# Turning and splitting the feed-forward's first block inside the attention's last block, in a Mamba-2 and ternary feed-forward layer on one core

## The reference

```python
x = L0_attn_u
x = _layernorm(x + _L0_attn_ref(x, ...), axis=-1)
x = _layernorm(x + _L0_ffn_ref(x, ...), axis=-1)

# attention (state space): z, x, B, C, dt from one projection; 8 heads of 128
xBC = silu(conv4(xBC));  dt = softplus(dt + bias)
y = ssd(x, dt, A, B, C, D)              # decays, states carried along the sequence
yg = y * silu(z)
yn = yg * rsqrt(mean(yg * yg) + eps) * norm_w
out = yn @ W_out.T

# feed-forward: weights are made ternary (-1, 0, 1 times the mean magnitude)
up, gate = x @ wu.T, x @ wg.T           # 512 -> 2048
out = (silu(up) * gate) @ wd.T          # 2048 -> 512
```

## Time and profile before

| | us |
|---|---|
| median of 3 runs | 1473.99 (1472.82 to 1474.25) |
| profiled execution, its own time | 1469.2 |
| its span | 1467.5 |
| TensorE busy | 1372.1 |
| VectorE busy | 1147.3 |
| ScalarE busy | 799.3 |
| GpSimd busy | 636.7 |

### The profile page before, as it was taken

One profiled execution on the slowest core, in us unless ns is written; L12 is line 12 of the kernel. 1 busy time (PEld: TensorE's weight loads), 2 busy tenths in 40 slices (PEclk: granted clock), 3 DMA queues, 4 the chain that ended last, 5 costly groups with the idle time before them and its releaser, 6 DMA issues.

```text
span 1467.5 us, 27103 instructions
## 1 busy us (share of the span) xinstructions
PE 1372.1 (94%) x9514; PEld 883.9 (60%) x9514; DVE 1147.3 (78%) x1844; ACT 799.3 (54%) x1592; POOL 636.7 (43%) x628
## 2 busy tenths in 40 slices
PE   6897999999999999999977989999999999999997
PEld 3454555555555656556555667676777767677773
DVE  6886787887778878788656887878797978888884
ACT  5685474773756738567364454454454544454440
POOL 0573354573655737446334333343342433333331
PEclk9899999999999999999987999999999999999999
DMA  7455325363453634425361120110101010110001
GB/s 257 111 191 164 111 77 129 85 162 91 95 148 80 155 88 105 137 73 151 112 217 32 37 96 28 44 37 23 59 29 59 30 45 30 44 44 30 27 27 64
DMA packets 138007, 129.11 MB, mean 88 GB/s; under 512 B 40336, under 2 KB 110352, under 8 KB 136592
## 3 DMA queue, kind: packets, MB, share of 16 engines
q1 hardware_dynamic: 137872, 127.35, 29.6%
HBM read 99.93 MB, written 27.39 MB: 87 GB/s over the span
## 4 chain that ended last, share of the span: by engine, by line
PE 35%; DVE 26%; issue 19%; ACT 11%; POOL 4%; DMA 4%; SPq 1%; DVEq 0%; ACTq 0%; POOLq 0%
PE ring L1008 7%; PE ring L810 5%; PE ring L837 5%; PE p_turn L992 4%; PE p_y L992 3%; DVE acc L1642 3%; PE p_seg L992 3%; PE p_st L992 2%; ACT p_seg L1203 2%; ACT xdt L1194 2%; DVE xdt L1949 2%; PE p_y L881 2%; DVE xdt L1957 2%; PE p_y L889 1%; ACT grow L1356 1%
## 5 line engine op out<-in xcount | busy, mean ns | idle before, releaser
L810 PE MATMUL ring<-u_split,weights 128*128 128x512 f16 x1620 | 376.9, 383 | 0.4 <-DVE x_ch L1647 0.4
L810 PEld LDWEIGHTS ring<-u_split,weights 128*128 128x128 f16 x1620 | 155.5, 99 | 171.4 <-issue 9.4
L1560 POOL TENSOR_TENSOR xdt<-xdt 128x512 f32<-128x512 f32 x64 | 81.4, 1273 | 291.0 <-DVE xdt L1957 291.0
L1642 DVE SCALAR_TENSOR_TENSOR acc<-ring,taps,acc 128x511 f32<-128x511 f32 (+2 forms) x192 | 143.7, 748 | 4.5
L837 PE MATMUL ring<-w_out,raw 128*128 128x512 f16 x672 | 147.1, 379 | 0.0
L1194 ACT ACTIVATE xdt<-p_turn,dts 128x128 f32<-128x128 f32 x256 | 73.0, 376 | 88.6 <-PE p_turn L861 88.6
L1469 POOL TENSOR_TENSOR raw<-yg,raw 128x512 f16<-128x512 f32 x64 | 79.4, 1241 | 87.2 <-ACT raw L1224 86.6
L837 PEld LDWEIGHTS ring<-w_out,raw 128*128 128x128 f16 x672 | 65.8, 99 | 77.7
L1464 POOL TENSOR_TENSOR yg<-y_ch,z_ch 128x512 f32<-128x512 f32 x64 | 82.4, 1288 | 58.6 <-DVE y_ch L1762 58.6
L1356 ACT ACTIVATE grow<-xdt,tanh_scale 128x512 f32<-128x512 f32 x64 | 46.2, 722 | 94.8 <-DVE xdt L1949 94.7
L881 PE MATMUL p_y<-seg,xdt 128*128 128x128 f32 x512 | 72.1, 286 | 18.3 <-DVE seg L1740 18.0
(11 more groups left out here) (383 smaller groups left out, 3435.9 us busy)
## 6 DMA issues: line engine op xcount, KB each, us to landing
cum_rows<-cum_dram SPq DMA_DIRECT2D x64, 256.0 KB, 6.5
quant<-in_w_ffn SPq DMA_DIRECT2D x24, 512.0 KB, 4.6
quant<-in_w_ffn SPq DMA_DIRECT2D x48, 256.0 KB, 4.2
u_raw<-in_u_t SPq DMA_DIRECT2D x8, 1024.0 KB, 13.0
cum_g<-cum_dram SPq DMA_DIRECT2D x64, 128.0 KB, 6.9
rows<-in_u_tok SPq DMA_DIRECT2D x32, 256.0 KB, 4.6
x_dram<-rows SPq DMA_DIRECT2D x32, 256.0 KB, 2.0
tern_ug<-quant SPq DMA_DIRECT2D x32, 256.0 KB, 3.5
```

Of the source, the lines that this page charges most:

```text
L810: mm = pe.matmul(bank_k[:, :], w_in[:, ws, k, col:col + P], us[:, par, k * T:(k + 1) * T], start=(i == 0), stop=(i == 3 * KD - 1))
L1560: pool.tensor_tensor(tile_[:, 1, :, :], tile_[:, 0, :, :], tile_[:, 1, :, :], ALU.mult).then_inc(hid_ok, 1)
L1642: dve.scalar_tensor_tensor(acc[:, buf, k + 1:T], own[:, 0:T - 1 - k], taps[:, h, 2 - k:3 - k], acc[:, buf, k + 1:T], ALU.mult, ALU.add).th ...
```

## The change

**The first block is turned in step 7.** On TensorE the four `turn` of block 0 leave the hand-over. Four `turn_first(k)` do the same transposes, into `p_turn`, one after each `chunk_out` at p = 1 of step 7. ScalarE reads them (`turned_first`) into `x_first`, which is the half of `u_hi` and `u_lo` that step 7 doesn't use.

**It is split in step 7.** The seven `x_high` of block 0 stand at p = 1 (j = 0, 1, 2), p = 2 (3), p = 3 (4 and 5) and in the hand-over (6); the `x_low` and the four `x_sum` on VectorE at p = 2 and p = 3, the last `x_low` in the hand-over. Block 0 has the set of buffers that block 1 had, and the other way round (`XS_AT`).

**The hand-over is filled.** TensorE does `last_chunk(0, 0)` and `last_chunk(1, 0)` there (they need heads 0 to 3 of y alone, and the waits say so), and the seven products of q = 0, before and after `outputs`. For q = 0 of block 0 the chain's bank is `ring[0]`. `ffn_step(-1)` starts with q = 1. ScalarE does all four `gated` before it.

**In step -1** the other half chunks stand in q = 1 to 4 (they stood in q = 1 to 5), block 1 is turned in q = 2 and 3 (was 0 and 1) and split in q = 4 to 7 (was 2 to 6), the sums of squares go to q = 2.

**At the start of the program** VectorE makes `w_lo(4)` after head 3's convolution (was before it), and `cb_tanh` and `cb_silu` of block 1 stand in place 2 of step 0 (were before it). SP issues `load_cum(1, 1, 1)` after the first two `load_abs` of step 1 (was before them).

Tables and the chain's bank:

```diff
-USES_LAST = ["x00", "x01", "x10", "x11", "ssq", "x20", "x21", "x30", "x31"]
+USES_LAST = ["x00", "x01", "x10", "x11", "ssq", "t0", "t1", "t2", "t3", "x20", "x21", "x30", "x31"]
...
+X_AT_FIRST = {4: (0,), 5: (1, 2), 6: (3, 4), 7: (5, 6)}
...
+        def p_chain(n, q):
+            return ring[0] if is_at(n, 0) and q == 0 else (p_st, p_seg)[q % 2]
```

SP, in the attention step:

```diff
                     if p == 0:
-                        load_cum(n, par, 1)
+                        if not is_at(n, 1):
+                            load_cum(n, par, 1)
...
                     if first_row is not None:
                         load_abs(first_row + 2)
                         load_abs(first_row + 3)
+                    if is_at(n, 1) and p == 0:
+                        load_cum(n, par, 1)
```

TensorE, in the attention step:

```diff
                         for c in range(1, C):
+                            if is_at(n, NB - 1):
+                                turn_first(c - 1)
                             chunk_out(n - 1, c)
+                    if p == 1 and is_at(n, NB - 1):
+                        turn_first(C - 1)
```

TensorE, in the hand-over:

```diff
             turn_x(NB, 0, 0)
-            turn(0, 0)
+            last_chunk(0, 0)
             turn_x(NB, 0, 1)
-            turn(0, 1)
+            last_chunk(1, 0)
             states(NB, 0)
-            turn(0, 2)
+            pe.wait_ge(tern_in[0], 16)
+            pe.wait_ge(xlo_ok, 7)
+            product(0, 0, 0, 1, True)
+            pe.wait_ge(s1_ok, 1)
+            product(0, 0, 0, 6, False)
+            pe.wait_ge(turn_free, turn_use(NB, "x01") + 1)
+            product(0, 0, 0, 5, True)
             outputs(NB, 0, 0)
-            turn(0, 3)
+            pe.wait_ge(u2_ok, 1)
+            product(0, 0, 0, 7, False)
+            pe.wait_ge(y_ok, NB * H - 1)
+            product(0, 0, 0, 2, True)
+            pe.wait_ge(y_ok, NB * H)
+            product(0, 0, 0, 4, True)
```

TensorE, in `ffn_step`:

```diff
-                    half = 2 * q - 3 if is_at(t, -1) and 1 <= q < 6 else None
+                    first, second = {1: (None, (0, 1)), 2: (None, (1, 1)), 3: ((2, 0), (2, 1)),
+                                     4: ((3, 0), (3, 1))}.get(q, (None, None)) if is_at(t, -1) else (None, None)
```

ScalarE, in the attention step:

```diff
+                    if is_at(n, NB - 1) and p >= 2:
+                        x_high(0, 0, p + 1)
...
+                    if is_at(n, NB - 1):
+                        for j in ((), (0, 1, 2), (), (5,))[p]:
+                            if j == 0:
+                                for k in range(KD):
+                                    turned_first(k)
+                            x_high(0, 0, j)
```

VectorE, at the start of the program:

```diff
-            w_lo(4)
             conv(0, 0, 3)
...
-            magnitude(1)
             dt_first(1, turn_use(0, "dt"))
+            w_lo(4)
+            magnitude(1)
             w_lo(5)
```

VectorE, in the attention step:

```diff
+                    if is_at(n, NB - 1) and p >= 2:
+                        for j in ((0, 1), (4,))[p - 2]:
+                            x_low(0, 0, j)
+                            x_sum((0, 1, None, None, 3)[j])
...
+                    if is_at(n, NB - 1) and p >= 2:
+                        for j in ((2, 3), (5,))[p - 2]:
+                            x_low(0, 0, j)
+                        if p == 2:
+                            x_sum(2)
```

More of the change, by code:

```diff
@@ L530, in rest, with splits_at, turns_at @@
             return (t, q // 2 - 1) if q else (t - 1, C - 1)
+        def splits_at(t, q):
+            return (X_AT_FIRST if is_at(t, -1) else X_AT).get(q, ()) if has_turn(t) else ()
+        def turns_at(t, q):
+            k = q - 2 if is_at(t, -1) else q
+            return k if has_turn(t) and 0 <= k < 2 else None
         def attention_rest(t, q):
@@ L710, in _ @@
             sp.wait_ge(z_full, NB * H)
+            sp.wait_ge(xlo_ok, 7)
             for q in (4, 5):
@@ L906, in _, with turn_first @@
             pe.wait_ge(made, 4)
+            def turn_first(k):
+                if k == 0:
+                    pe.wait_ge(xin_in, 16)
+                pe.wait_ge(turn_free, turn_use(NB - 1, f"t{k}"))
+                for c in range(C):
+                    mm = pe.transpose(p_turn[:, c * P:(c + 1) * P], u_raw[:, c * D + k * P:c * D + (k + 1) * P], ident[:, :])
+                mm.then_inc(turn_full, 1)
             dt_proj(0, 0, 0)
@@ L1589, in ffn_step @@
             def ffn_step(t, par):
-                for q in range(NQ):
+                for q in range(1 if is_at(t, -1) else 0, NQ):
                     before = pair_at(t, par, q, 1)
@@ L1812, in ffn_scales, with x_low, x_sum @@
                 dve.wait_ge(scale_ok, 2)
+            def x_low(n, par, j):
+                dve.wait_ge(xhi_ok, n * 7 + (j + 1))
+                dve.tensor_tensor(xs_lo[par][j], place(n, SPLIT[j]), xs_hi[par][j], ALU.subtract).then_inc(xlo_ok, 1)
+            def x_sum(k):
+                if k == 0:
+                    dve.wait_ge(turn_free, turn_use(NB - 1, "t3") + 1)
+                else:
+                    dve.wait_ge(xt_ok, k)
+                dve.wait_ge(xlo_ok, (1, 1, 4, 2)[k])
+                a_, b_, c_ = SUMS[k]
+                dve.tensor_tensor(place_first[a_], place_first[b_], place_first[c_], ALU.subtract).then_inc(xt_ok, 1)
             dve.memset(ones, 1.0)
@@ L1877, in step @@
                         within(n, par, p, 0)
+                    if first and p == 2:
+                        cb_silu(1, 1, ring[ring_bank("cb", 0)])
                     if not end:
@@ L1931, in _ @@
             run_steps(dve, step)
-            def x_low(n, par, j):
-                dve.wait_ge(xhi_ok, n * 7 + (j + 1))
-                dve.tensor_tensor(xs_lo[par][j], place[SPLIT[j]], xs_hi[par][j], ALU.subtract).then_inc(xlo_ok, 1)
             def summed(n, q, c, kept, kept_ok, j, op):
@@ L2005, in _ @@
             dve.wait_ge(scales_ok, 3)
-            x_low(0, 0, 0)
-            x_sum(0)
-            x_low(0, 0, 1)
-            x_sum(1)
-            x_low(0, 0, 2)
             skip(NB, 1, 0)
             skip(NB, 1, 1)
-            x_low(0, 0, 3)
-            x_sum(2)
-            x_low(0, 0, 4)
-            x_sum(3)
-            x_low(0, 0, 5)
-            x_low(0, 0, 6)
+            summed(0, 0, "c11", s1, s1_ok, 2, ALU.add)
             def ffn_step(t, par):
                 n, own = t + 1, 1 - par
-                for q in range(NQ):
+                for q in range(1 if is_at(t, -1) else 0, NQ):
                     before, earlier = pair_at(t, par, q, 1), pair_at(t, par, q, 2)
```

226 lines of the change are left out of this document (118 added, 108 removed).

## The result

The changed kernel takes 1460.48 us (median of 4 runs, 1459.47 to 1463.34), the one before 1473.46 (1472.82 to 1474.25): a ratio of 0.9915, 95% interval 0.9898 to 0.9932, so 13.0 us or 0.85% less. The forecast was 1457, 17 us less, with a range of 1448 to 1467.

A forecast was written before the change was run, and what follows sets the result against it. TensorE, busy 94% of the span, was taken as the bound, so gains come only where it idles or runs at the lower clock. 10.8 (after step -1) - 0.8 (clock) + 7.0 (start) = 17 us: 1474 to 1457, range 1448 to 1467.

The forecast's parts named there:

- (a): Step 7: the four turns between the chunks only change place, 4 x 0.44 = 1.8 us.
- (b): Step 7, end of p = 1: `turn_x` waits about 0.9 us for ScalarE's read; 1.2 us more in all, between 0 and 3.
- (c): Step 7, places 2 and 3: VectorE's added instructions delay convolutions; first four 3.7 us, 2.4 us lost at `x_dt`, 1.7 at the mask.
- the mask of place 3: Step 7: TensorE's `within` of the second head has no slack and loses 1.7 us waiting for the mask.
- My 0.8 us for the clock: Step -1: taken off the gain because TensorE would be idle some 6 us in q = 5.
- 14.0: Hand-over: q = 0 done 9.65 us earlier, with two half chunks (5.2) and two turns (0.9) less left to do: 14.0 us won.
- (d): Start: `w_lo(4)` moved from ahead of head 3's convolution, which TensorE's mask wait follows; 2.4 us gained, bounds 0 and 4.
- (e): Start: magnitude piece issued ahead of `load_cum`, so ScalarE's 9.43 us wait shrinks; 4.3 us gained, between 0 and 9.43.
- R1: Half the gain: VectorE slower in step -1 (5.7 us less) or piece no earlier (4.3 less); 1462 or 1467; 27% with R4.
- R2: More: splits find VectorE's gaps, step 7 pays 2 us instead of 5.3, piece lands 7 us earlier; 23 us, 1451; 18%.
- R3: Slower: clock falls to 1.2 GHz through places 2 and 3 of step 7, up to 30 us more; 1487 at worst; 5%.
- R4: Hand-over: `xlo_ok` so late that products stand after `outputs` as before, and `outputs` waits too; 12 us, 1462; 27% with R1.

The follow-up runs named there:

- halves_back: Changed kernel with both half chunks taken out of the hand-over, into q = 1 and q = 2 of step -1: 1463.0 us, ratio 0.9924 to before.
- u_mid: Changed kernel with `load_u(2)` issued behind step 1's two magnitude pieces but ahead of `load_cum(1, 1, 1)`: 1457.9 us, ratio 0.9899 to before.
- after_again: The changed kernel, unaltered, timed once more beside later runs: 1459.1 us, ratio 0.9906 to before.
- feed_only: Changed kernel with the start of the program as it was before: 1465.9 us, ratio 0.9945 to before.
- cum_first: Changed kernel with `load_cum(1, 1, 1)` ahead of the magnitude pieces again: 1461.4 us, ratio 0.9915 to before.
- u_late: Changed kernel with the 1 MB `load_u(2)` issued behind step 1's magnitude pieces and `load_cum`, not ahead of `store_cum`: 1454.4 us, ratio 0.9861 to before.
- thin_last: Changed kernel with block 1's splits and sums in step -1 cut to 2 columns of 512 (block 1's result wrong): 1453.4 us, ratio 0.9861 to before.
- start_only: The kernel before with only the start's part of the change: 1467.8 us, ratio 0.9961 to before.
- combo: Changed kernel with the edits of `u_late` and `splits_behind` together: 1453.2 us, ratio 0.9852 to before.
- thin_step7: Changed kernel with block 0's splits and sums cut to 2 columns of 512 (block 0's result wrong): 1457.0 us, ratio 0.9885 to before.
- splits_behind: Changed kernel with step 7's splits and sums behind the second head's convolution, `x_high(3)` and `x_high(4)` behind its tanh: 1455.6 us, ratio 0.9881 to before.

## Why the prediction was right

On the clock of before (2.06 us added to the rows after), step by step:

| step (us) | predicted | after |
|---|---|---|
| step 7 ends (`turn_x` behind the last z tile) | 758.5 | 758.5 |
| half chunk (0, 0) begins | 761.4 | 761.6 |
| half chunk (1, 0) begins | 766.4 | 766.6 |
| product 1 begins | 772.4 | 772.9 |
| `outputs` ends | 779 | 780.6 |
| q = 0 done | 781.6 | 783.3 |
| product 3 in q = 1 | 784.7 | 786.6 |
| in q = 4 | 818.6 | 820.5 |
| in q = 5, 6, 7 | 829.2, 841.9, 850.9 | 831.7, 843.4, 853.5 |
| first of step 0 | 860.2 | 862.5 |

**Step 7.** The sum of 7 us held (6.7). (a) The turns cost their 1.8. (b) `turn_x` waited 0.78 us for ScalarE's read, not 0.9. (c) At place 2 the four instructions took 4.4 us in place of 3.7:

```profile
731.50 0.68 DVE L1893 TENSOR_TENSOR xs_more<-u_split,xs_more 128x512 f16<-128x512 f32 x1
732.28 1.46 DVE L1903 TENSOR_TENSOR u_split<-u_split 128x512 f32<-128x512 f32 x1
733.66 1.75 DVE L1893 TENSOR_TENSOR xs_more<-u_split,xs_more 128x512 f16<-128x512 f32 x1
735.34 0.68 DVE L1903 TENSOR_TENSOR u_split<-u_split 128x512 f32<-128x512 f32 x1
```

```profile
731.69 1.50 POOL L1546 TENSOR_TENSOR raw<-yg,raw 128x512 f16<-128x512 f32 x1 [0.69 <-ACT raw L1277]
733.15 1.71 POOL L1554 TENSOR_TENSOR sq_sum<-sq_sum,sq 128x512 f32<-128x512 f32 x1
```

The two long ones meet two long ones on GpSimd; VectorE's other two took 0.68. I had said that GpSimd has a gap there, and it hadn't. The Trainium skill (SBUF — State Buffer, section "SBUF: two separate sides") has the two engines lock a shared pair of ports, and these rows agree: GpSimd's instructions grow too, from 1.16 and 1.27 us. `x_dt` was late by 2.71 us (2.4 predicted). The trace after shows no wait for the mask of place 3, to which I gave 1.7 us, and a tile slowed by 1.7 us (4.44 for 2.75) in its place. It would be wrong to read this as a term that wasn't there. `halves_back` has the same tile at full clock and then the wait, 1.21 us, and loses the same 6.7 us in sum, so the mask was the limit as I had said, and the lower clock ran beside it.

**The hand-over.** Every start up to product 1 is within 0.5 us. The starts wait for VectorE: z's gate ends at 764.48 and half chunk (1, 0) begins at 764.53, the last split ends at 770.68 and product 1 begins at 770.83. So the 1.5 us that half chunk (0, 0) took longer cost nothing. What failed is the clock behind product 1, for which I let each instruction take its full-clock time. Two products took 0.8 and 0.45 longer, which nothing hid, and with the 0.5 by which product 1 was late they make the delay of 1.6 to 1.9 us that stands from `outputs` to q = 4. My 0.8 us for the clock were for q = 5. So the gain there was 12.3 us, not 14.0.

`u_mid`, which differs only at the start of the program, shows what the step is worth without it, as its products ran at full clock behind the same wait:

```profile
765.91 1.03 PE L1033 MATMUL ring<-xs_more,weights 128*128 128x256 f16 x8 [2.51 <-DVE b_tok L1892]
...
778.38 1.05 PE L1033 MATMUL p_turn<-c_ch,weights 128*128 128x256 f16 x8 [1.37 <-DVE xdt L2046]
```

From product 1 to product 3 of q = 1 that is 12.5 us. I had 12.3 (772.4 to 784.7), the trace after has 13.7, and `after_again`, `feed_only`, `cum_first`, `u_late` and `thin_last`, with the same order there, have 15.1 to 15.3. The term that I left out is worth 0 to 3 us, from one execution to the next.

**Step -1.** That VectorE sets the pace in q = 4 to 7 is shown by `thin_last`, and it gave back 3.8 us against 3.2. The single terms were less good than the sum: from q = 4's product 3 to step 0's first they were 11.2, 11.8, 10.0 and 9.0 us against 10.6, 12.7, 9.0 and 9.3, and in q = 4 TensorE did not wait for VectorE, where I had said every q.

**Net** 8.5 us in the trace and 8.1 by `feed_only`, against 10.8 - 0.8 = 10.0. Reckoned in the same way, five more traces with this order give 6.6 to 9.8, and the 9.8 is `u_mid`'s.

**The start** gained 5.8 us by `start_only`, predicted 7.0, but by other terms. (d) I took 2.4 us. At 109.03 of before, ahead of the long wait, the lead is 2.2 in the trace after, 3.4 in `start_only`'s and 3.5 in `cum_first`'s, and 1.7 to 4.4, 3.2 on average, in all twelve traces with this start: some 0.8 us more than I took. (e) I took 4.3. The traces give 2.7: TensorE's wait for `x_dt` was 8.9, 9.1 and 9.6 us in the three with `load_cum` first, and 4.6 to 7.8, 6.5 on average, in the eight with the piece first. The timed runs of `cum_first` give 0 to 1.3 and can't decide. The step that failed says that the piece's way "is as long at worst (less was moved ahead of it)". It was longer in seven traces of eight, by 2 us on average; that the `load_cum` issued just ahead of it is the reason is argued, not shown. With 3.2 and 2.7 the sum is 5.9, and 5.8 was measured: a term too small and one too large made my 6.7, and that the sum was near is in part luck. The sign that I named for it, a wait of 5 us or less on ScalarE, came in none of the eight (5.09 to 8.36, 7.65 in the trace after).

**The rivals.** R1 (half) holds in part, as the piece came less early than I took, and the median of 1460.5 lies at the upper end of the forecast's own 1453 to 1461, just below R1's 1462; its other half, 12 us each in q = 6 and 7, didn't come (10.0 and 9.0). R2 didn't come, as step 7 paid 6.7 us. R3 didn't come: the clock in places 2 and 3 fell to 0.95 only, and that cost nothing at the end of step 7. R4 didn't either: `xlo_ok` came 2.51 us late, and `outputs` didn't wait.

## What to carry to other kernels

Filler work on an engine goes behind the instruction that the critical path waits for, not ahead of it: moved behind the convolution (and ScalarE's part behind the tanh), the whole splits cost no more, up to product 1, than splits cut to two columns ahead of it. When work is moved into idle time, a step behind a wait of 2.5 us has two prices, at full and at the lower clock, and belongs in the sum as a range; where another engine's instruction comes later anyway, the slow clock is free. And a load that is late is moved by what stands in the queue ahead of it: look for the large load that delays a small store on which others wait. A stretch that DMAs set is priced from several traces, since one trace here was off by 2 us and more.

## What the runs showed of the hardware

ScalarE's piece, the first of two loads of 512 KB, took 6.2 to 6.9 us from issue to landing in the three traces with the megabyte behind it (`u_late`, `u_mid`, `combo`), 9.3 to 9.6 in the three with both `load_cum` ahead of it, and 9.1 to 12.8 in eight traces with one `load_cum` just ahead. What is issued around it moves it, and so does something that differs between executions of the same order.

TensorE's granted clock after short waits: half chunks behind 1.24 and 1.25 us of idle time (`thin_step7`) and behind 1.47 us (`splits_behind`) took the 2.76 us of full speed, 2.4 GHz; behind 2.56 us one took 4.29, most of it at 1.2 GHz. But the length of the wait doesn't decide alone. Behind the same wait of 2.71 to 2.73 us in step 7 a tile took 4.44 us in the changed kernel and 2.75 in `halves_back`; product 1 behind 2.51 us took 1.84 and 1.03 (`u_mid`); and a product behind 3.40 us (`thin_last`) took 1.05.

A 16 KB store issued half a microsecond behind a 1 MB load delayed the load that waits for it to 6.4 to 7.2 us after the store's issue in eleven traces; without the megabyte that was 4.3 to 4.4 us in three (4.41 in `u_late`, 98.21 to 102.62).

A VectorE instruction of 128x512 on two SBUF inputs takes 0.68 or 0.69 us alone; two that met GpSimd's took 1.46 and 1.75, and GpSimd's grew from 1.16 and 1.27 (at 731.05 and 732.17 of before) to 1.50 and 1.71.
